# A Mamba and mixture-of-experts block on one core: ScalarE's piece copies, VectorE's side steps and the first half of dt change places

## The reference

```python
x = x + conv_ref(ln_c(x))        # a Mamba block over a pixel-shuffled image, 4 x 512 x 24 x 24
t = tokens(x)
t = t + ffn_ref(ln_t(t))         # 8 experts, top 2, and one shared expert
# inside conv_ref: L = 2304 steps (and one token), 256 channels, 16 states
xz = seq @ in_proj.T;  u, z = split(xz);  u = silu(conv4(u))
dt, B, C = split(u @ x_proj.T)
dt = softplus(dt @ dt_proj.T + b)
h = exp(dt * A) * h + (dt * u) * B          # the scan over time, per channel and state
y = (h . C) + u * D;  y = y * silu(z);  out = y @ out_proj.T
# inside ffn_ref, the shared expert: silu(x @ sw1) * (x @ sw3) @ sw2
```

## Time and profile before

| what | number |
|---|---|
| median of three runs | 2363.06 us |
| the profiled execution | 2365.38 us |
| its span, first to last instruction | 2363.6 us |
| busy over the span: PE, POOL, DVE, ACT | 90%, 52%, 55%, 44% |
| first scan-stage instruction on VectorE | 73.38 us |
| end of the last scan | 1231.4 us |
| mean granted clock of TensorE | 0.934 |

### The profile page before, as it was taken

One profiled execution on the slowest core, in us unless ns is written; L12 is line 12 of the kernel. 1 busy time (PEld: TensorE's weight loads), 2 busy tenths in 40 slices (PEclk: granted clock), 3 DMA queues, 4 the chain that ended last, 5 costly groups with the idle time before them and its releaser, 6 DMA issues.

```text
span 2363.6 us, 30197 instructions
## 1 busy us (share of the span) xinstructions
PE 2116.5 (90%) x8172; PEld 1141.4 (48%) x8173; DVE 1298.8 (55%) x2036; ACT 1038.7 (44%) x2114; POOL 1219.8 (52%) x1132
## 2 busy tenths in 40 slices
PE   5667778989889899898878999999999999999995
PEld 4223335555555555555446844444444444444443
DVE  2799999999989999999983411111111111111112
ACT  3787788877778777887732111101101101101100
POOL 3699998999889999899870001111111111111110
PEclk8678789999989999999989999999999999999996
DMA  5555655556545565555635231413132313141116
GB/s 191 145 143 142 160 141 139 145 136 155 149 129 137 143 155 144 142 144 140 159 93 197 90 120 19 132 27 125 26 93 61 130 27 126 24 133 22 23 22 169
DMA packets 156887, 271.71 MB, mean 115 GB/s; under 512 B 16800, under 2 KB 103944, under 8 KB 154192
## 3 DMA queue, kind: packets, MB, share of 16 engines
q1 hardware_dynamic: 147120, 247.61, 36.5%
q0 software_dynamic: 9632, 22.55, 5.2%
HBM read 222.58 MB, written 51.71 MB: 116 GB/s over the span
## 4 chain that ended last, share of the span: by engine, by line
PE 56%; issue 11%; ACT 10%; DVE 8%; POOL 8%; DMA 6%; SPq 1%; POOLq 0%; ACTq 0%; DVEq 0%
PE pair L1836 21%; PE single L1848 13%; PE pair L1557 7%; DVE WALL L1269 6%; POOL WALL L710 4%; DMA u<-xrows,gix 3%; PE pair L1563 3%; ACT WALL L993 2%; PE single L1475 2%; PE pair L1676 2%; ACT L796 1%; DMA WALL<-yrows 1%; POOL sp L608 1%; PE single L1512 1%; PE pair L1819 1%
## 5 line engine op out<-in xcount | busy, mean ns | idle before, releaser
L710 POOL TENSOR_TENSOR WALL<-WALL 128x768 f32<-128x768 f32 x384 | 694.6, 1814 | 50.9 <-DVE WALL L1269 39.3
L1269 DVE TENSOR_TENSOR_SCAN WALL<-WALL,carry,pair 128x384 f32<-128x384 f32 x640 | 610.2, 992 | 0.0
L1836 PE MATMUL pair<-WALL,zz 128*128 x1376 | 597.8, 592 | 2.0 <-ACT zz L1093 1.1
L993 ACT ACTIVATE WALL<-WALL,AnR 128x384 f32<-128x384 f32 x768 | 425.3, 605 | 48.1 <-DVE WALL L1269 32.6
L771 POOL DMA_INDIRECT yrows<-sp,aix x43 | 68.9, 1601 | 688.7 <-ACT sp L1105 671.0
L1836 PEld LDWEIGHTS pair<-WALL,zz 128*128 128x128 f32 x1376 | 258.1, 190 | 311.0 <-issue 311.0
L1423 DVE SCALAR_TENSOR_TENSOR sp<-XA,tab,pair 128x512 f32<-128x512 f32 x86 | 64.3, 747 | 567.0 <-ACT XA L1099 567.0
L1557 PE MATMUL pair<-XA,WALL 128*128 128x288 f32 x1024 | 298.1, 442 | 48.3 <-ACT XA L908 39.9
L1848 PE MATMUL single<-WALL,sp 128*128 x688 | 303.1, 593 | 2.7 <-issue 1.5
L1099 ACT ACTIVATE XA<-pair 128x512 f32<-128x512 f32 x86 | 51.4, 597 | 577.6 <-PE pair L1836 577.6
L1557 PEld LDWEIGHTS pair<-XA,WALL 128*128 128x128 f32 x1024 | 205.0, 205 | 127.3 <-issue 43.6
(11 more groups left out here) (262 smaller groups left out, 2261.2 us busy)
## 6 DMA issues: line engine op xcount, KB each, us to landing
WALL<-dtd SPq DMA_DIRECT2D x384, 192.0 KB, 3.9
WALL<-in_L_ffn_w_dram SPq DMA_DIRECT2D x24, 2048.0 KB, 13.8
WALL<-wsd SPq DMA_DIRECT2D x144, 256.0 KB, 3.2
WALL<-crows SPq DMA_DIRECT2D x96, 192.0 KB, 4.1
dtd<-sp SPq DMA_DIRECT2D x96, 192.0 KB, 2.8
WALL<-wsd SPq DMA_DIRECT2D x16, 768.0 KB, 4.6
X<-in_x_dram SPq DMA_DIRECT2D x4, 1152.0 KB, 6.5
xrows<-rows SPq DMA_DIRECT2D x24, 192.0 KB, 2.8
```

The lines of the kernel that those rows point to most:

```text
L710: pool.tensor_tensor(hC[m], hs[:, (NS * j + n) % HRING, :, :], Cs[k][:, n % NPH // 2, :].unsqueeze(1).to_broadcast([P, HALF, T]), ALU.mult ...
L993: a = nsc.activation(dA[(NS * j + n) % AHEAD][:, e, :], dtR[:, h * NQ + c + e, :], ACT.Exp, scale=AnR[:, c + e, h, q:q + 1])
L1269: scan = nv.tensor_tensor_scan(hs[:, m, e, :], dA[(NS * j + n) % AHEAD][:, e, :], dBu[e], init, ALU.mult, ALU.add)
L1836: last = mm(bank[2 * w + q][:, :], xT[k][:, r, :], WALL[:, ds(off + (w * RR * I + r * I + q * 512), 512)], start=(r == 0), stop=(r == RR - 1))
```

## The change

Three edits, in four places.

```diff
+        H1_INSIDE = (0, 3)
...
@@ SyncE, ahead of the stage @@
             for h in range(HALF):
                 store_dt(0, 0, h)
                 spread_dt(0, 0, h)
-            for h in range(HALF):
                 store_dtu(0, 0, h)
                 spread_dtu(0, 0, h)
...
@@ GpSimd, softplus_tail: the product of half h waits for half h alone @@
                     if h == 0:
-                        pool.wait_ge(f_dt, HALF * (g + 1))
                         pool.wait_ge(f_u, 2 * g + 2)
+                    pool.wait_ge(f_dt, HALF * g + h + 1)
...
@@ GpSimd, ahead of the stage @@
+            for n in (3, 4, 7, 5, 6, 8):
+                softplus_tail(n, 0, 0)
             front_centre(2, 0, 2)
-            for n in range(NS):
-                softplus_tail(n, 0, 0)
...
@@ ScalarE, in exps, ahead of the load back @@
+                if shared_group is not None:
+                    h1_copy(shared_group, H1_INSIDE[1], E1)
                 exp_and_ln()
...
@@ ScalarE, in batch @@
-                                if phase == H1_OUT[q] // NS and n == H1_OUT[q] % NS:
+                                if q not in H1_INSIDE and phase == H1_OUT[q] // NS and n == H1_OUT[q] % NS:
                                     h1_copy(G, q, E1)
...
+                            if not first and j % GC == 0:
+                                h1_copy(group_of(b, j), H1_INSIDE[0], E1)
                             exp_and_ln()
...
-                            exps(g + 1)
+                            exps(g + 1, shared_group=group_of(b, j) if not first and j % GC == 0 else None)
...
@@ VectorE, in batch: the wait for dA and the two scans move ahead of the three side steps @@
+                        v.wait_ge(m_dA, i + 1)
+                        after(v, m_hC, i - HRING + 1)
+                        after(v, m_carry, NPAIR * g + (n - HRING) // 2 + 1)
+                        for e in range(2):
+                            ...
+                            scan.then_inc((m_h0, m_h)[e], 1)
                         if front and n == 1:
                             residue(g + 1, 1 - k)
                         if not first and j % GC == 1 and n in GATED_AT:
...
                             nv.tensor_tensor(xv, xv, E1, ALU.add).then_inc(e_y, 1)
-                        v.wait_ge(m_dA, i + 1)
...
```

More of the change, by code:

```diff
@@ L837, in abs_relu, with exps @@
                    .then_inc(f_abs, 1)
-            def exps(g, with_exp=None, with_ln=None):
+            def exps(g, with_exp=None, with_ln=None, shared_group=None):
                 sc.wait_ge(f_abs, 2 * g + 2)
@@ L1252, in batch @@
                         nv.tensor_tensor(dBu[1], dtuR[:, h * NQ + c + 1, :], Bq[:, 0:T], ALU.mult).then_inc(m_dBu, 1)
+                        v.wait_ge(m_dA, i + 1)
+                        after(v, m_hC, i - HRING + 1)
+                        after(v, m_carry, NPAIR * g + (n - HRING) // 2 + 1)
+                        for e in range(2):
+                            init = (h0 if j == 0 else carry)[:, n, e:e + 1]
+                            v.wait_ge((m_dBu0, m_dBu)[e], i + 1)
+                            scan = nv.tensor_tensor_scan(hs[:, m, e, :], dA[(NS * j + n) % AHEAD][:, e, :],
+                                                         dBu[e], init, ALU.mult, ALU.add)
+                            scan.then_inc((m_h0, m_h)[e], 1)
                         if front and n == 1:
```

## The result

The changed kernel takes 2333.8 us (median of four runs, 2330.0 to 2336.1) against 2363.0: a ratio of 0.9873, 95% interval 0.9856 to 0.9891. It is faster, and inside the range that was given, but 17 us above the predicted 2317. The profiled execution took 2333.4 us, its span 2331.6.

The account below looks back on a forecast made before the run. VectorE was taken as nearest the bound, GpSimd and TensorE 3 to 4 us behind per group. -8.9 - 25.6 - 28.0 + 14 = -48.5 from 2365.4 gave 2317 us, range 2303 to 2340.

Parts of the forecast that it names:

- the first rival: Scan stage: GpSimd and TensorE set the pace, half the copies' and side steps' gain returns; 2330 us (2325 to 2342), chance 0.30.
- the first dBu: Start of the scan stage: first dBu at 64 to 65 us, not 73.
- the up-1 piece: Up-1 chunks: no 4-us TensorE wait before L1557, and a piece of about 2.1 us there.
- the spread waits: Scan stage: VectorE's dBu waits for the spread at L1666 fall from 21.4 to below 5 us.
- One sign of being wrong: Behind the scans: the forecast is wrong if that stage is longer than 1132 us.
- Term 1: Ahead of the scan stage: reordered stores and spreads, centring behind dt steps, start the first dBu sooner; -8.9 us (-3.0 to -11.4).
- term 3: Scan stage: VectorE's side steps (additions, residue, gates) moved behind the scans, which fill their waits; -28.0 us.
- Term 2: Up-1 chunks: earlier copy of piece 3 brings TensorE's spread sooner, removing VectorE's spread waits; -25.6 us (other end 12).
- Given back: Scan stage: new waits for GpSimd, for TensorE and where the image loop turns; +14 us, between 0 and 30.
- Copy 0 at nothing: Earlier copy of piece 0 saves TensorE a 2.02-us wait but no VectorE wait; booked at nothing.
- The copies do not reach the spread: TensorE's piece 4 held by something else, so mainly the gain ahead of the stage remains; 2352 us, chance 0.08.
- TensorE goes cold behind the gates: Up-2 and down chunks: later gates make TensorE wait and run pieces at half clock; slower, 2398 us, chance 0.04.

Follow-up runs that it names:

- all four pairs of the table: Kernels alike but for side steps moved behind the scans; copies old or inside, centring at 10 or 8: 2358.0/2337.2, 2357.0/2333.8, 2351.5/2331.9, 2336.2/2314.9 us.

## Why the prediction was right, and where it was not

The range held, but not its likeliest part. 2333.8 lies above the 2303 to 2325 that had 0.55, in the stretch given to the first rival, which the range was drawn wide enough to take in; and what kept the time there is, for the most part, not what that rival says. Of the signs on record, the first dBu, the up-1 piece and the spread waits came. The side steps' waits did not fall below 8 us (28.0), and the group shown took 143.5 us, not 140 to 143. One sign of being wrong came too, 1133.5 us behind the scans instead of 1132; but the kernels here, whose work behind the scans is the same, show 1131.7 to 1133.5 there, so it tells nothing.

**Term 1, -8.9, right.** The first dBu after, which answers to the last of the earlier trace rows:

```profile
64.66 0.56 DVE L1254 TENSOR_TENSOR pair<-WALL,pair 128x384 f32<-128x384 f32 x1 [1.38 <-DMA WALL<-dtd]
```

64.66 against the 64.5 worked out. "I book nothing" for the centring that moves to 56 was right only because term 3 covers it: 2.1 us in the kernel without term 3.

**Term 2, -25.6, is the step that failed, with its share of "Given back".** Its first half is right to the row: no 4-us wait ahead of piece 4, a warm up-1 chunk (clock 1.00, was 0.90), 21.6 of the 25.6 us of spread waits gone. What failed is the last step, from waits that vanish to time that is won. Alone or with the side steps, the copies brought 1 us by the time and 4 to 6 by the stage (1161.4 to 1157.3, 1139.3 to 1133.5). In the up-1 chunks alone they brought 23, close to what was booked; 17 to 18 of it were lost in the up-2 chunks. Under "Given back" I booked GpSimd by its busy time, "0.5 us a group, 3 in all", and the whole at 14. The stage gave 24.5 where the two terms had 53.6: given back were 29, at the end of its range ("between 0 and 30"). What was late next was, for the most part, not an engine without time but one step of it, the centring, which ends a wait of ScalarE. That wait was in the trace before the change, 54.4 us in 21 pieces, and I did not read it, as ScalarE had 10 of 49 us idle.

**Term 3, -28.0, right in kind, 22 in size.** 19 to 22 us in all four pairs of the table. It looked like nothing in the profile after, whose side steps wait 28.0 us as before.

**Copy 0 at nothing: right**, by the run without it.

**The rivals.** *GpSimd and TensorE set the pace* has the time (2330, within 2325 to 2342) but not most of the mechanism: with all work of both engines kept and one step of GpSimd moved by two states, the kernel takes 2314.9. The scans wait for nothing, before and after. A smaller part is the rival's: less work on either engine also shortens chunks that the centring leaves as they are. *The copies do not reach the spread*: they do. *TensorE goes cold behind the gates*: of 144 pieces in the stage the trace counts 11 that ran at a mean granted clock below 0.8, where there were 24; the point from which it decides was 38. Six of the 11 stand behind the late dtr, one in each up-2 chunk after a wait of 3.2 to 3.3 us, and one directly behind a wait for a gate (0.13 us). By the rule of the Trainium skill's page "TensorE: Matmul & The Clock Gate", section "HAM oscillation — how this bites in real kernels", slow starts could have followed one another; the trace shows single ones, as the one at 825.62, and the stage's mean clock rose from 0.90 to 0.92.

## What to carry to other kernels

The sum of one engine's waits for one cause says how long it stood there, not what removing the cause is worth: follow who is late next, on the engines off the path too, and look there for waits that are already long. When two edits stand together, the profile after can credit the wrong one: run each alone. And a step of a filled engine is priced by where it stands in that engine's order, before its busy time: here one number, with no work added or taken, was worth as much as the move of all side steps once the copies stood inside, and 5 to 6 us without them.

## What was not expected of the hardware

Taking work from TensorE made the rest of its work slower in sum. Groups of TensorE in the scan stage (busy us, mean ns of one, idle before), the changed kernel:

```profile
L1479 PE MATMUL single<-seq,Wu 128*128 128x384 f32 x352 | 141.8, 537 | 0.1
L1567 PE MATMUL pair<-XA,WALL 128*128 128x288 f32 x384 | 104.8, 417 | 3.2 <-DVE XA L1167 2.2 <-DVE X L1275 1.1
...
L1474 PE MATMUL pair<-WALL,meanw 128*128 128x96 f32 x344 | 47.3, 281 | 0.0
```

and the one with half of the convolution's products:

```profile
L1567 PE MATMUL pair<-XA,WALL 128*128 128x288 f32 x384 | 115.7, 450 | 2.7 <-DVE XA L1167 1.7 <-DVE X L1275 1.1
L1479 PE MATMUL single<-seq,Wu 128*128 128x384 f32 x176 | 81.4, 564 | 0.0
...
L1474 PE MATMUL pair<-WALL,meanw 128*128 128x96 f32 x344 | 56.2, 316 | 0.0
```

The convolution (L1479) lost 60.4 us, but TensorE's busy time in the stage fell only from 981.6 to 938.7, by 42.9. The other lines together took 17.5 us more: the two shown went from 417 to 450 and from 281 to 316 ns each, most lines stayed as they were, and one went the other way (the dt product L1516, 648 to 576 ns). The stage's mean granted clock was 0.90 where it had been 0.92, and over the whole span 0.930 to 0.935 in five runs against 0.940 to 0.944 in four. One step shows how. With less of its own to do TensorE waits longer for GpSimd's products (in front of L1680 87.1 us in the stage, 47.3 in the changed kernel), and in this step what stands behind the wait ran at the lower clock, 0.50:

```profile
811.22 0.87 PE L1680 MATMUL pair<-WALL,fold 128*32 128x384 f32 x8 [3.06 <-POOL WALL L710]
...
812.02 2.02 PE L1474 MATMUL pair<-WALL,meanw 128*128 128x96 f32 x8
```

```profile
812.02:814.04 2.02, 2.02 (x13) 2.02 (x10) 0.04 (x1) 2.01 (x4) 2.02 (x3) 0.50 0.57 202
```

In the changed kernel the same eight products stand behind a wait of 1.13 us, start at 814.62 and take 1.13 us at a granted clock of 1.00. So nearly a third of the work saved (17.5 of 60.4 us) went into slower products of the rest.
